# Sort by source: the last 96 of 416 steps placed by scattered transfers into a blanked array, the first 320 by products

## The chip, the cores and the metric

One core of a Trainium2 chip runs the whole program. The metric is the device time of one execution in microseconds. Engines go by the profile's short names: PE (TensorE, matrix products; PEld its weight loads), DVE (VectorE), ACT (ScalarE), POOL (GpSimd) and SP (SyncE, which mostly issues DMAs here).

## The reference

Four graph layers on 3125 nodes of 256 features and 53125 edges, cut to what matters here:

```python
x = layernorm(x + L0(x, src, dst, ...))          # max over the edges of each source node, 3 times
x = layernorm(x + L1(x, edge_index, type, weight, ...))   # relational layer, sum over the edges of each target, 2 times
x = layernorm(x + L2(x, edge_index, ...))        # normalised graph convolution
x = layernorm(x + L3(x, src, dst, ...))          # attention over the edges, then a feed-forward part
# in L0:
xi, xj = x[src], x[dst]
e = relu((xj - xi) @ theta.T + xi @ phi.T)
agg = jax.ops.segment_max(e, src, num_segments=N)
```

Nothing is said on the order of the edges, which come sorted by target. For the maximum over the edges of a source the kernel sorts them by source on the chip, and then walks along them.

## The kernel before

**The layout.** The edges are padded to SLOTS = 128 x 416 = 53248. An array of one value per edge lies in SBUF as 128 partitions x STEPS = 416 columns; edge number e is at partition e // 416 ("block"), column e % 416 ("step").

**The sort by source** is a counting sort. `edge_order` (from L204) compares and counts (L227 to L341, up to about 313 us), then looks up for each edge the place that it gets in the sorted order (the phase from L386, 313 to 405 us; its loops are on DVE, ACT and PE alone). `node_ends` (from L483) finishes the places in a run of short DVE instructions, each waiting for the one before: `place` is a number of 0 to 53247 for each edge, and `locate` splits it into `blk` (place // 416) and `stp` (place % 416). No two edges have the same place.

**The placing.** `permute` (from L531) then moves what is to be sorted, the other end's node number in two pieces (`env.piece`: number >> 8 and number & 255), to its place by matrix products. For each of the 416 columns t of the unsorted array, a one-hot matrix `hot_step` (128 x 416, L562) has the new column of the partition's edge, and for each piece a matrix `marked_piece` (128 x 128) has the piece's value at the new partition. Their product, added up in PSUM over all t (L607, banks 0 and 1), is the sorted array: in each element one of the 53248 summands isn't zero. `BySource.place_edges` (L704 to L714) joins the two banks to `self.row` = 256 x bank 0 + bank 1.

The columns are taken in groups of four (`group` = 4), in a ring of four groups. DVE makes for each group four `hot_step`, three `hot_block` (L565) and the fourth column's two `marked_piece` (L569); ACT makes the other three columns' six `marked_piece` (L589); PE does eight products (L607). DVE waits for `used` from four groups back, ACT for `hot`, PE for `hot` and `marked`. Each engine loops with `over_groups`. With 416 columns that is 104 groups, 26 rounds of the ring. POOL and SP have no work in this phase.

`permute` is called a second time in `node_ends`, for the ends of the nodes (25 columns, groups of one). `segments` and everything later follow.

**What sets the order.** Each `phase` ends with a barrier of all engines, then a block in which POOL resets the DMA state and clears the phase's semaphores one by one (L74), so no work of one phase overlaps with that of the next.

The array `flat`, a scratch tensor of 2 x SLOTS 4-byte elements in HBM, is used later by `StepOrder` only.

## Time and profile before

| | |
|---|---|
| median of 3 runs | 7662.52 us (7645.81 to 7680.71) |
| profiled execution | 7700.27 us |
| its span in the profile | 7698.5 us |
| PE busy | 3055.6 us (40%) |
| DVE busy | 3786.4 us (49%) |
| ACT busy | 1760.0 us (23%) |
| POOL busy | 3188.1 us (41%) |
| `permute` of the edges | 418 to 618 us of the span |
| granted clock of PE, mean | 0.685 |

Busy time is that of instructions on an engine; matmuls are pipelined and their ends modelled. All rows below are of one profiled execution, with times in microseconds from the span's start. "Idle before" is how long the engine stood still before an instruction, and what follows the arrow is what ended that. An instruction with "issue" there waited for nothing that the profile shows. DVE and ACT instructions overlap with the next of their engine, so the time from one start to the next is shorter than the duration. A DMA issued by POOL shows as DMA_INDIRECT, which is the time in which POOL makes the descriptors; the data move later.

### The profile page before, as it was taken

To read this page: it belongs to the slowest core of one execution; us is meant where nothing else is said; L and a number is where in the kernel's file an instruction comes from. 1 tells how busy PE (TensorE), PEld (TensorE's weight loads), DVE (VectorE), ACT (ScalarE), POOL (GpSimd) and SP (SyncE) were. 2 spreads that over 40 slices of the span, in tenths; PEclk is the share of its full clock that TensorE was granted. 3 is DMA by queue.
4 is the path that set the end of the run, shared out by engine and by line. 5 is a ranking of instruction groups with operands and counts; after the bars stand their busy time and mean duration, and the time that the engine had idled before them with its cause. 6 is when DMAs were issued, how large, how long until landed. Compare 5 with 4: busy or idle time off the path is not lost. (4 is left out here: it accounts for less than half of the span.)

```text
span 7698.5 us, 78156 instructions
## 1 busy us (share of the span) xinstructions
PE 3055.6 (40%) x12869; PEld 1815.1 (24%) x12895; DVE 3786.4 (49%) x9263; ACT 1760.0 (23%) x4531; POOL 3188.1 (41%) x3220
## 2 busy tenths in 40 slices
PE   4474000433335545689200199000200035666638
PEld 3332000221113222334100044000100024545415
DVE  8995445344444555544333444333543354555451
ACT  1182000021112444321222211222200011222211
POOL 0003666434443655300566400666366644444520
PEclk9997555655557777789655599555555558887769
DMA  0003455333333444333345333455245536777630
GB/s 7 0 0 99 163 168 176 102 107 128 124 127 103 142 144 152 111 113 149 134 172 172 133 146 137 151 175 175 102 148 184 173 114 202 252 246 246 214 79 17
DMA packets 376598, 1056.27 MB, mean 137 GB/s; under 512 B 73683, under 2 KB 161141, under 8 KB 329877
## 3 DMA queue, kind: packets, MB, share of 16 engines
q0 software_dynamic: 164688, 466.32, 20.4%
q1 hardware_dynamic: 210450, 587.55, 20.0%
q10 hardware_dynamic: 1330, 0.99, 0.0%
q8 instruction: 43, 0.70, 0.0%
q14 instruction: 87, 0.70, 0.0%
HBM read 537.47 MB, written 517.10 MB: 137 GB/s over the span
## 5 line engine op out<-in xcount | busy, mean ns | idle before, releaser
L912 POOL DMA_INDIRECT rows<-typed_table,index x832 | 826.9, 994 | 1324.1 <-DVE index L936 1085.8
L912 POOL DMA_INDIRECT out_of<-table,index x936 | 940.8, 1005 | 955.1 <-DVE index L936 679.0
L912 POOL DMA_INDIRECT rows<-table,index x728 | 722.6, 993 | 466.3 <-DVE index L936 242.5
L1086 PE MATMUL bank<-ident,tail 128*128 128x128 f32 x6 | 2.0, 434 | 1850.4 <-PEq L74 1850.4
L2276 PE MATMUL bank<-weights,out_of 128*128 128x512 f32 x1600 | 699.8, 595 | 26.7 <-DVE weights L2324 26.7
L2680 POOL DMA_INDIRECT qv<-qv_table,index x416 | 421.5, 1013 | 455.2 <-DVE index L2880 330.2
L930 ACT ACTIVATE rows<-rows,by_target_weight 128x256 f32<-128x256 f32 x832 | 345.7, 495 | 941.1 <-DMA rows<-typed_table,index 863.5
L951 DVE SCALAR_TENSOR_TENSOR y<-y,by_source_anew,out_of 128x256 f32<-128x256 f32 x897 | 434.1, 484 | 214.8 <-issue 86.5
L1806 PE MATMUL bank<-x,marks 128*128 128x416 f16 x1664 | 379.7, 389 | 390.7 <-ACT marks L1820 330.3
L1820 ACT ACTIVATE marks<-hot_block,x 128x128 f16<-128x128 f16 x1248 | 370.7, 387 | 409.6 <-DVE marks L1861 388.6
L951 DVE SCALAR_TENSOR_TENSOR out_of<-out_of,by_target_keep,rows 128x256 f32<-128x256 f32 x598 | 290.4, 486 | 306.4 <-issue 187.1
L1086 PEld LDWEIGHTS bank<-ident,tail 128*128 128x128 f32 x6 | 0.9, 203 | 1852.4 <-issue 1852.4
L2276 PEld LDWEIGHTS bank<-weights,out_of 128*128 128x128 f32 x1600 | 305.6, 191 | 391.4 <-issue 389.0
L2757 PE MATMUL bank<-weighed_rows,hot 128*128 128x272 f32 x832 | 283.6, 466 | 183.5 <-ACT y L2855 100.8
L2897 DVE TENSOR_TENSOR qv<-qv,bank 128x512 f32<-128x512 f32 x208 | 141.8, 685 | 377.6 <-remote 152.7
L2296 DVE COPY staged<-bank 128x512 f32<-128x512 f32 x200 | 138.4, 692 | 371.5 <-PE bank L2276 371.5
L1806 PEld LDWEIGHTS bank<-x,marks 128*128 128x128 f16 x1664 | 177.8, 109 | 592.6 <-issue 505.1
L951 DVE SCALAR_TENSOR_TENSOR state<-state,by_target_keep,rows 128x256 f32<-128x256 f32 x273 | 132.5, 485 | 366.2 <-issue 242.8
L2745 PE MATMUL bank<-near,y 128*128 128x256 f32 x832 | 253.1, 445 | 147.5 <-DMA near<-k_rows 108.0
L2296 ACT COPY staged<-bank 128x512 f32<-128x512 f32 x200 | 117.2, 586 | 637.6 <-PE bank L2276 637.6
L2855 ACT COPY y<-bank 128x272 f32<-128x272 f32 x416 | 153.5, 387 | 469.1 <-PE bank L2757 187.5
L1940 POOL MEMSET floor<- 128x256 f32 x1 | 0.3, 312 | 615.4 <-POOLq L74 615.4
(509 smaller groups left out, 6962.3 us busy)
## 6 DMA issues: line engine op xcount, KB each, us to landing
states<-y SPq DMA_DIRECT2D x156, 1024.0 KB
typed_table<-staged SPq DMA_DIRECT2D x400, 256.0 KB, 2.0
states<-state SPq DMA_DIRECT2D x78, 1024.0 KB
states<-out_of SPq DMA_DIRECT2D x78, 1024.0 KB
wide_states<-y SPq DMA_DIRECT2D x52, 1088.0 KB
near<-k_rows SPq DMA_DIRECT2D x416, 128.0 KB
out_of<-table,index POOLq DMA_INDIRECT x936
rows<-typed_table,index POOLq DMA_INDIRECT x832
```

Source lines behind the costliest of these rows:

```text
L912: pool.indirect_dma_start(out=rows[h][:, u * D:(u + 1) * D], out_offset=None, in_=table, in_offset=bass.IndirectOffsetOnAxis(ap=index[h][: ...
L930: nc.scalar.activation(row, row, ACT.Copy, scale=order.weight[:, bass.ds((RING * i + h) * GROUP + u, 1)]).then_inc(weighed, 1)
L951: nc.vector.scalar_tensor_tensor(out=state[h][:, u * D:(u + 1) * D], in0=before, scalar=marks[:, bass.ds(g * GROUP + u, 1)], in1=rows[h][: ...
L1806: last = nc.tensor.matmul(env.bank[i][:, 0:STEPS], self.marks[h][i][:, u * P:(u + 1) * P], self.hot_step[h][:, u * STEPS:(u + 1) * STEPS], ...
L1820: last = nc.scalar.activation(self.marks[h][i][:, u * P:(u + 1) * P], self.hot_block[h][:, u * P:(u + 1) * P], ACT.Copy, scale=self.pieces ...
L2276: last = nc.tensor.matmul(bank[:, 0:pair], turned_y[:, a * D + s * P:a * D + (s + 1) * P], weights[h][:, s * pair:(s + 1) * pair], start=s ...
L2296: copy(staged[m % slots][:], env.bank[a % banks][:, 0:pair]).then_inc(read, 1)
L2680: pool.indirect_dma_start(out=qv[b][:, u * PAIR:(u + 1) * PAIR], out_offset=None, in_=qv_table, in_offset=bass.IndirectOffsetOnAxis(ap=ind ...
L2745: last = nc.tensor.matmul(env.bank[k % 2][:, j * D:(j + 1) * D], hot_turned[h][:, u * P:(u + 1) * P], near[h][:, u * D:(u + 1) * D], start ...
L2757: nc.tensor.matmul(env.bank[2 + j][:, 0:ROW], hot[b % RING][:, u * P:(u + 1) * P], weighed_rows[b % 2][:, u * ROW:(u + 1) * ROW], start=Tr ...
L2855: nc.scalar.copy(staged[h][:, u * ROW:(u + 1) * ROW], env.bank[2 + u % 2][:, 0:ROW]).then_inc(kept, 1)
L2897: nc.vector.tensor_tensor(out=q, in0=q, in1=by_step(env.bank[k % 2][:], D, 2), op=ALU.mult).then_inc(multiplied, 1)
```

## The change

The first 320 columns of the unsorted array are placed by products as before (BY_PRODUCT). The last 96 go another way. In the look-up phase POOL blanks a tile, and SP stores it over the first SLOTS elements of `flat` (`slots`), 208 KB. `node_ends` makes two more tiles of 96 columns with DVE: `spot`, the place as a whole number, and `value`, 256 x piece 0 + piece 1. In the `permute` phase POOL issues 96 indirect DMAs, one for each of the columns; each sends 128 elements of 4 bytes, one of a partition, to their places in `slots`. SP waits for all of them (semaphore `scattered`), loads `slots` into the tile `scattered_in` and waits for that. `place_edges` then adds `scattered_in` to PSUM bank 1 where it copied bank 1 before. Both calls of `permute`, and the look-up phase, get two more semaphores each.

```diff
@@ -201,7 +201,10 @@
                 then(nc.vector.tensor_copy(env.piece[1][:], part[:]))
 
 
-def edge_order(nc, env, order, target, given):
+BY_PRODUCT = 320
+
+
+def edge_order(nc, env, order, target, given, slots):
 
 
 
@@ -381,9 +384,20 @@
             part = buffer(inner, nc, "part", 2 * W1)
             high_low = buffer(inner, nc, "high_low", 2 * W2, BF16)
             found = buffer(inner, nc, "found", 2 * W2)
-            names = ("added", "cut_high", "cut", "looked_up", "picked", "placed", "held")
-            with phase(nc, *names) as (added, cut_high, cut, looked_up, picked, placed, held), \
+            blank = buffer(inner, nc, "blank", STEPS)
+            names = ("added", "cut_high", "cut", "looked_up", "picked", "placed", "held", "blanked", "cleared")
+            with phase(nc, *names) as (added, cut_high, cut, looked_up, picked, placed, held, blanked, cleared), \
                     nc.Block() as block:
+                @block.gpsimd
+                def _(pool):
+                    pool.memset(blank[:], 0.0).then_inc(blanked, 1)
+
+                @block.sync
+                def _(sp):
+                    sp.wait_ge(blanked, 1)
+                    sp.dma_start(slots.rearrange("(p t) o -> p (t o)", t=STEPS), blank[:]).then_inc(cleared, 16)
+                    sp.wait_ge(cleared, 16)
+
                 def part_of(h):
                     return bulk(part[:, h * W1:(h + 1) * W1], GROUP)
 
@@ -477,10 +491,10 @@
         counting.close()
 
 
-        node_ends(nc, env, order, place, rank)
-
-
-def node_ends(nc, env, order, place, rank):
+        node_ends(nc, env, order, place, rank, slots)
+
+
+def node_ends(nc, env, order, place, rank, slots):
 
 
     with ExitStack() as inner:
@@ -491,6 +505,8 @@
         l_blk, l_stp = si("l_blk", TILES), si("l_stp", TILES)
         last, crosses = si("last", TILES), si("crosses", TILES)
         blk, stp = si("blk", STEPS), si("stp", STEPS)
+        spot = buffer(inner, nc, "spot", STEPS - BY_PRODUCT, I32)
+        value, scattered_in = si("value", STEPS - BY_PRODUCT), si("scattered_in", STEPS)
         with phase(nc, "step") as (step,), nc.Block() as block:
             @block.vector
             def _(dve):
@@ -507,6 +523,9 @@
                 then(nc.vector.tensor_tensor(out=place[:], in0=place[:], in1=blk[:], op=ALU.mult))
                 then(nc.vector.tensor_scalar(out=place[:], in0=place[:], scalar1=ROUND, scalar2=-ROUND, op0=ALU.add, op1=ALU.add))
                 then(nc.vector.scalar_tensor_tensor(out=place[:], in0=place[:], scalar=-1.0, in1=rank[:], op0=ALU.add, op1=ALU.subtract))
+                then(nc.vector.tensor_copy(spot[:], place[:, BY_PRODUCT:]))
+                then(nc.vector.scalar_tensor_tensor(out=value[:], in0=env.piece[0][:, BY_PRODUCT:], scalar=256.0, in1=env.piece[1][:, BY_PRODUCT:],
+                                                    op0=ALU.mult, op1=ALU.add))
                 locate(place, blk, stp)
                 locate(order.start, n_blk, n_stp)
                 then(nc.vector.tensor_scalar(out=order.some[:], in0=order.count[:], scalar1=1.0, scalar2=None, op0=ALU.min))
@@ -523,12 +542,12 @@
                 then(nc.vector.scalar_tensor_tensor(out=l_blk[:], in0=l_blk[:], scalar=1.0, in1=crosses[:], op0=ALU.add, op1=ALU.mult))
                 then(nc.vector.tensor_scalar(out=order.end_block[:], in0=l_blk[:], scalar1=-1.0, scalar2=None, op0=ALU.add))
 
-        order.place_edges(nc, env, place, blk, stp)
+        order.place_edges(nc, env, place, blk, stp, (spot, value, slots, scattered_in))
         permute(nc, env, n_blk, n_stp, [order.some], TILES, 1)
         segments(nc, env, order)
 
 
-def permute(nc, env, blk, stp, pieces, tiles, group):
+def permute(nc, env, blk, stp, pieces, tiles, group, scatter=None):
 
     n = len(pieces)
     body = RING * group
@@ -550,7 +569,23 @@
         hot_step = buffer(stack, nc, "hot_step", body * STEPS, BF16)
         hot_block = buffer(stack, nc, "hot_block", body * P, BF16)
         marked_piece = buffer(stack, nc, "marked_piece", body * n * P, BF16)
-        with phase(nc, "hot", "marked", "used", "held") as (hot, marked, used, held), nc.Block() as block:
+        with phase(nc, "hot", "marked", "used", "held", "scattered", "reloaded") as (hot, marked, used, held, scattered, reloaded), nc.Block() as block:
+            if scatter is not None:
+                spot, value, slots, scattered_in = scatter
+                many = STEPS - tiles
+
+                @block.gpsimd
+                def _(pool):
+                    for t in range(many):
+                        pool.indirect_dma_start(out=slots, out_offset=bass.IndirectOffsetOnAxis(ap=spot[:, t:t + 1], axis=0),
+                                                in_=value[:, t:t + 1], in_offset=None).then_inc(scattered, 16)
+
+                @block.sync
+                def _(sp):
+                    sp.wait_ge(scattered, 16 * many)
+                    sp.dma_start(scattered_in[:], slots.rearrange("(p t) o -> p (t o)", t=STEPS)).then_inc(reloaded, 16)
+                    sp.wait_ge(reloaded, 16)
+
             @block.vector
             def _(dve):
                 def make(g, h):
@@ -703,13 +738,13 @@
 
 class BySource(Order):
 
-    def place_edges(self, nc, env, place, blk, stp):
-        permute(nc, env, blk, stp, env.piece, STEPS, 4)
+    def place_edges(self, nc, env, place, blk, stp, scatter):
+        permute(nc, env, blk, stp, env.piece, BY_PRODUCT, 4, scatter)
         with phase(nc, "step") as (step,), nc.Block() as block:
             @block.vector
             def _(dve):
                 then = counted_steps(dve, step)
-                then(nc.vector.tensor_copy(env.tmp[:], env.bank[1][:, 0:STEPS]))
+                then(nc.vector.tensor_tensor(out=env.tmp[:], in0=env.bank[1][:, 0:STEPS], in1=scatter[3][:], op=ALU.add))
                 then(nc.vector.scalar_tensor_tensor(out=self.row[:], in0=env.bank[0][:, 0:STEPS], scalar=256.0, in1=env.tmp[:],
                                                     op0=ALU.mult, op1=ALU.add))
 
@@ -3342,7 +3377,7 @@
             edge_buffers(inner, nc, env)
             env.piece = [buffer(inner, nc, f"piece{i}", STEPS) for i in range(2)]
             edge_columns(nc, env, given["src"], given["dst"])
-            edge_order(nc, env, by_source, by_target, given)
+            edge_order(nc, env, by_source, by_target, given, flat[0:SLOTS, :])
         by_source.end_row, by_target.end_row = (buffer(stack, nc, "end_row", ROWS, BF16) for _ in range(2))
         steps = StepOrder(stack, nc, env, by_source, by_target, flat, window_table, k_rows)
         x, y = buffer(stack, nc, "x", TILES * D), buffer(stack, nc, "y", TILES * D)
```

## Rows read from the trace of the kernel before

**Rows 1.** Busy time by stage: stretch, length, busy and count per engine, clock, DMA.

```profile
core 0: us, PE busy (x) PEld busy (x) DVE busy (x) ACT busy (x) POOL busy (x), PEclk, DMA share, GB/s
313.00:405.50 92.50, 56.69 (x416) 42.41 (x416) 81.27 (x208) 19.20 (x52) 0.00 (x0) 1.00 0.00 0
418.00:616.00 198.00, 163.04 (x824) 73.77 (x824) 196.01 (x936) 193.28 (x624) 0.00 (x0) 1.00 0.00 0
```

**Rows 2.** Groups, 417.5 to 618 us: busy, mean ns of one, idle before, releasers.

```profile
L589 ACT ACTIVATE marked_piece<-hot_block,piece 128x128 bf16<-128x128 bf16 x624 | 193.4, 389 | 21.6 <-DVE marked_piece L569 19.1 <-issue 0.4
L607 PE MATMUL bank<-hot_step,marked_piece 128*128 128x416 bf16 x832 | 164.6, 342 | 49.4 <-ACT marked_piece L589 49.3
L562 DVE TENSOR_SCALAR hot_step<-iota_steps,stp 128x416 bf16<-128x416 f16 x416 | 133.7, 321 | 0.9 <-PEq L74 0.9
```

**Rows 3.** Timeline of the placing stage: start, duration, instruction, idle before it.

```profile
418.04 0.33 DVE L562 TENSOR_SCALAR hot_step<-iota_steps,stp 128x416 bf16<-128x416 f16 x1 [0.92 <-PEq L74]
...
500.49 0.53 DVE L569 TENSOR_SCALAR marked_piece<-iota_p,blk,piece 128x128 bf16<-128x128 bf16 x2
...
502.38 0.53 DVE L569 TENSOR_SCALAR marked_piece<-iota_p,blk,piece 128x128 bf16<-128x128 bf16 x2
...
616.26 1.57 PE L607 MATMUL bank<-hot_step,marked_piece 128*128 128x416 bf16 x8 [0.32 <-ACT marked_piece L589]
618.74 0.59 DVE L712 COPY tmp<-bank 128x416 f32<-128x416 f32 x1 [4.69 <-PEq L74]
```

**Rows 4.** Groups of GpSimd, whole span: a 4-byte gather, a 1 KB scatter.

```profile
L2547 POOL DMA_INDIRECT k_rows<-staged_k,step_place x25 | 24.7, 988 | 39.1 <-DVEq L2607 39.1
L2685 POOL DMA_INDIRECT ahead<-window_table,step_step_in x25 | 24.0, 962 | 7.6 <-issue 7.6
```

**Rows 5.** DMA: queue over 7284 to 7288 us (packets, MB, share); issues (KB, landing us).

```profile
q0 software_dynamic: 93, 0.00, 1.7%
...
typed_table<-staged SPq DMA_DIRECT2D x400, 256.0 KB, 2.0
...
weights<-in_L_gnn_thetas SPq DMA_DIRECT2D x3, 256.0 KB, 2.8
```

**Rows 6.** L1857 beside and without indirect DMAs: timeline, line (min/median/max), group.

```profile
2613.29 2.25 DVE L1857 TENSOR_SCALAR x<-iota_steps,x 128x416 f16<-128x416 f16 x8
2614.50 0.94 POOL L912 DMA_INDIRECT out_of<-table,index  x1 [0.30 <-issue]
2622.26 1.17 POOL L912 DMA_INDIRECT out_of<-table,index  x1 [3.52 <-DVE index L936]
2622.51 1.98 DVE L1857 TENSOR_SCALAR x<-iota_steps,x 128x416 f16<-128x416 f16 x8
3186.13 1.99 DVE L1857 TENSOR_SCALAR x<-iota_steps,x 128x416 f16<-128x416 f16 x8
...
L1857 DVE TENSOR_SCALAR x<-iota_steps,x x8: 310/323/518, 2613.3 to 2615.2; 128x416 f16<-128x416 f16 x8
...
L1857 DVE TENSOR_SCALAR x<-iota_steps,x 128x416 f16<-128x416 f16 x416 | 109.3, 334 | 0.0
```

**Rows 7.** Timeline: an indirect DMA beside a long DVE instruction.

```profile
744.78 1.49 POOL L912 DMA_INDIRECT out_of<-table,index  x1 [0.30 <-issue]
745.12 1.03 DVE L1457 TENSOR_SCALAR x<-tmp 128x416 bf16<-128x416 int32 x1
```

**Rows 8.** Timeline of node_ends: its first instruction, and two of 25 columns.

```profile
406.51 2.75 DVE L506 RECIPROCAL blk<-col_a 128x416 f32<-128x416 f32 x1 [1.09 <-PEq L74]
...
412.82 0.18 DVE L501 TENSOR_SCALAR n_blk<-by_source_start 128x25 f32<-128x25 f32 x1
413.04 0.18 DVE L502 TENSOR_SCALAR n_blk<-n_blk 128x25 f32<-128x25 f32 x1
```

**Rows 9.** Waits of SP's queue: total us, times, longest.

```profile
SPq L386 <- PEq L386: 92.1, 1, 92.1
SPq L74 <- PEq L74: 50.1, 44, 3.3
```

## The prediction

> **What bounds the stretch now.** I read the table of busy time by stage first, because an average over 7698.5 us says nothing of one stage. The change touches the sort of the edges by source, which fills the first 634 us. In its placing stage, 418 to 616 us, VectorE is busy 196.0 us of 198.0, ScalarE 193.3, TensorE 163.0 and GpSimd 0.0, and the DMA engines move nothing [rows 1]. The groups of instructions of this stage come next. ScalarE's 624 scalings are busy 193.4 us and wait 21.6 before them, 19.1 of which is the wait for the first group; TensorE waits 49.4 us for ScalarE [rows 2]. So TensorE isn't the bound. VectorE and ScalarE are, nearly tied, and neither waits for the other. The timeline has the pace. The last instructions of two groups of four steps, the pair of L569, start at 500.49 and 502.38 us, 1.885 us apart; a check over the stage gives the same: 196.0 / 104 groups = 1.885 [rows 1, 3]. ScalarE needs 193.4 / 104 = 1.86 us a group [rows 2]. The first L562 starts at 418.04, the last product starts 616.26 and ends 617.83, and the next instruction on VectorE follows at 618.74 [rows 3]. All later work waits for it, since every phase ends in a barrier. A microsecond saved here is a microsecond of the whole.
>
> **Part 1, fewer products.** 416 steps become 320, so 104 groups become 80 and the loop of 26 rounds of four groups becomes 20 without a rest. 24 groups x 1.885 us = **45.2 us** less, on VectorE and ScalarE alike, and TensorE's share goes with them (its eight products take 1.57 us of the 1.885) [rows 1, 3]. What would be next to bound the stage if these were cheaper doesn't matter: their pace per group stays.
>
> **Part 2, 96 scatters on GpSimd.** Each sends 128 values of 4 bytes. The trace has a near twin, L2685: 25 gathers of 4-byte elements, written out without a loop, 962 ns each with 7.6 / 25 = 0.30 us between them; a scatter exists too, L2547, 988 ns with rows of 1 KB [rows 4]. The time follows the count of 128 addresses and hardly the size or the direction, so one costs 0.96 + 0.30 = 1.26 us and 96 of them 121 us. GpSimd idles in this stage, so from 418.3 they are issued by 539. The reload of 208 KB follows. A load of 256 KB takes 2.8 us to land [rows 5], and the last scatter has to land before it, in some 2 us more (an estimate from the 2.0 us of a store there), so `reloaded` stands at about 544. The products end at 617.8 - 45.2 = 572.6 at the earliest. The scatters are hidden with 29 us to spare. They surface only if one costs more than (572.6 + 9.6 - 418.3 - 5) / 96 = 1.65 us, the 9.6 being part 3. SP, whose queue waits behind `scattered`, has nothing else queued until the phase's end.
>
> The transfers' own cost: four 4-byte gathers put 1.7% on the 16 engines in 4 us, 1.1 us of engine time over all of them, under 0.1 us per engine for four [rows 5]. The trace has no scattered 4-byte write into HBM. From below it costs what the gather does. From above it costs 2.0 us with no overlap, the time in which a 256 KB store lands [rows 5]. The gather is the nearer row, so I take hidden.
>
> The Trainium skill ("DMA: Bandwidth & Descriptors", Specifications) says that below 512 bytes a DMA engine reads, modifies and writes. No row here shows that for a 4-byte write; it is what would push toward the upper bound, which is rival B.
>
> **Part 3, what the scatters do to VectorE.** This is the term that I am least sure of. The stage has no GpSimd work now, so I looked where the same sort of VectorE instruction runs beside indirect DMAs. L1857 is the twin of L562: 128x416, 16 bits in and out, eight in a row. Undisturbed, eight take 1.99 us. At 2613.29 they take 2.25, and one of the eight lasts 518 ns where its median is 323; GpSimd's DMA of 2614.50 lies in the burst and takes 0.94 us, no longer than alone [rows 6]. So GpSimd gets through short VectorE instructions, and makes one of them wait 0.20 to 0.26 us at times. How often: over all 416, L1857's mean is 334 ns against 321 for L562, 13 ns x 416 = 5.4 us [rows 2, 6]. Starts in a burst are (1.99 - 0.32) / 7 = 0.24 us apart, so the bursts cover 100 us; at one DMA per 1.26 us that is at most 80, so at least 0.07 us each; leaving out the bursts in which GpSimd pauses, like 3186.13, it is nearer 0.10. I take 0.10 x 96 = **9.6 us**. Bounds: 0 (each DMA slips in between), and 0.25 x 96 = 24 us. A gain is excluded, as nothing gets faster by sharing. ScalarE has only 0.02 us a group of slack, so it can't take up the loss, and it is paid in full.
>
> What GpSimd suffers: beside a long VectorE instruction it does wait. The DMA of 744.78 takes 1.49 us and ends 0.12 us after the 1.03 us instruction of 745.12 [rows 7]. The stage's instructions last 0.25 to 0.33 us and the next overlaps them, so I expect 0 to 0.1 us of such waiting, 120 to 130 us for all 96. It changes no end.
>
> **Part 4, small ones.** Two more VectorE instructions of 96 columns in the node_ends phase: the 25-column ones start 0.22 us apart and those of 416 columns last 0.59 [rows 3, 8], so about 0.27 each, **0.5 us**. The blanking (a memset on GpSimd, a 208 KB store on SP) lies in the look-up stage of 92.5 us in which GpSimd and DMA idle and SP waits 92.1 us for TensorE [rows 1, 9]; memset and store are a few us at its start, so it costs nothing. Without that cover it would cost some 4 us. The sum from PSUM replaces a copy of the same shape, 0.59 us before and after [rows 3]. Semaphores: the phase with seven leaves VectorE idle for 1.09 us, that with one for 0.92 [rows 3, 8], 0.03 each. Three phases get two more: **0.2 us**. The barrier on GpSimd after a phase with DMAs could take longer: the 44 barriers take 1.14 us on average and 3.3 at the longest [rows 9], so up to 2 us, and I take 0.
>
> **Sum.** -45.2 + 9.6 + 0.5 + 0.2 = -34.9 us. The profiled execution took 7700.27 us, span 7698.5, so it would take 7665.4. The median of the three runs is 7662.52, 38 below the profiled one; the same difference gives **7628 us**. With part 3's bounds and part 4's 2 us the forecast's own range is 7618 to 7644.
>
> **Rivals.**
> D, no disturbance: GpSimd fits between VectorE's instructions. For it: the burst of 2622.51, beside the DMA of 2622.26, takes 1.98 us. Against: the 518 ns instruction [rows 6]. -44.5 us, 7618.
> B, the scatters surface: at 1.9 to 2.0 us each, by slow 4-byte writes or by waits like 744.78's all along, the reload ends at 418.3 + 192 + 4 = 614 and the stage saves only 4 us: 7659. At 1.8 us it would be 7640. For it: no row of such a write, and [rows 7]. Against: [rows 4] and the idle DMA engines.
> A, starvation, which ends slower: VectorE is busy all through the stage, 196.0 of 198 us, and if its instructions in the fast mode kept GpSimd from writing descriptors, the 96 scatters would come after the last of them: 418 + 151 of products + 121 + 5 = 695 instead of 617.8, +77 us, 7740. It decides from where a third of the DMAs are still to come when the products end (578 + 40 + 5 = 623). For it: the stage has no gap, whereas the bursts of the twin last 2 us. Against: 2614.50, wholly inside a burst, isn't held at all.
> The Trainium skill ("SBUF — State Buffer", Who interferes with whom) states exactly this rule: a VectorE instruction in a two-port mode holds the shared port pair for its whole length and GpSimd blocks, starved of descriptor writes. This trace agrees for the long instruction of 745.12 and disagrees for the short ones of 2613.29.
>
> **Chances.** Forecast 0.55, D 0.20, B 0.17, A 0.08. The range, 7608 to 7664, takes in the forecast, D and B with the spread of the runs, and leaves out A and the tails. 0.5% (38 us) is about what a measurement can tell from no change; the border is 7624. Faster: 0.16 of D and 0.14 of the forecast, 0.30. Slower: A, 0.08. Within: 0.62.
>
> **What would show it.** L562 320 times, its pace still 1.885 us a group once GpSimd is done (after about 540) and about 2.0 before: each DMA costs 0.10 and 1.5 of them fall in a group. L562's mean 325 to 345 ns. 96 indirect DMAs at 1.25 to 1.35 us from one start to the next. The next stage begins about 583 instead of 618.7, on a release by TensorE and not by SP. Wrong, if SP's wait for `scattered` ends last, or if the mean of the DMAs is above 1.3 us.

## The result

The changed kernel took 7706.0 us at the median against 7651.7 for the kernel before: a ratio of 1.0084, interval 1.0058 to 1.011 (the plain quotient of the two medians is 1.0071). The prediction was 7628 and a ratio of 0.9955; it had given a chance of 0.08 to any loss over 0.5%. On a second sort of chip, reached only late in the study, the same two kernels stand at 0.994 (0.9926 to 0.9953). Most of this section is about how one change can be both.

The profiled execution of the changed kernel took 7682.64 us, its span 7680.9. First, the groups of its placing stage, as [rows 2] for the kernel before: busy us, mean ns of one, idle before them and its releasers. L597 is the former L562, L624 the former L589, L642 the former L607, and L580 the new scatters.

```profile
L624 ACT ACTIVATE marked_piece<-hot_block,piece 128x128 bf16<-128x128 bf16 x474 | 146.8, 388 | 133.4 <-DVE marked_piece L604 128.7 <-issue 3.2
L642 PE MATMUL bank<-hot_step,marked_piece 128*128 128x416 bf16 x624 | 133.1, 362 | 144.1 <-ACT marked_piece L624 106.0 <-issue 19.2 <-DVE marked_piece L604 18.9
L597 DVE TENSOR_SCALAR hot_step<-iota_steps,stp 128x416 bf16<-128x416 f16 x320 | 100.2, 313 | 111.1 <-remote 77.8 <-issue 29.6 <-PE bank L642 2.9
L580 POOL DMA_INDIRECT flat<-value,spot x96 | 93.2, 971 | 134.4 <-POOLq L74 105.4 <-issue 29.0
```

ScalarE waits 128.7 us for VectorE, TensorE 106.0 for ScalarE, and VectorE 111.1 us for something that the profile can't name ("remote", "issue"). None of the three is busy most of the time while the scatters are issued. In [rows 1] VectorE and ScalarE had worked 196.0 and 193.3 of 198.0 us. By stretches (length, busy and count of each engine, granted clock, DMA share and GB/s), the first two with scatters, the third after them:

```profile
core 0: us, PE busy (x) PEld busy (x) DVE busy (x) ACT busy (x) POOL busy (x), PEclk, DMA share, GB/s
418.00:486.00 68.00, 19.78 (x72) 8.25 (x72) 17.91 (x81) 16.53 (x54) 51.09 (x53) 0.71 0.02 1
486.00:554.00 68.00, 8.79 (x24) 3.06 (x24) 7.53 (x34) 5.58 (x18) 42.13 (x44) 0.53 0.03 4
554.00:681.00 127.00, 104.54 (x528) 47.39 (x528) 126.73 (x606) 124.79 (x403) 0.00 (x0) 0.98 0.00 0
```

Before 554 us, some 13 of the 80 groups of products are made in 136 us; after it, the other 67 in 127 us, 1.89 us each, the pace of before. The stage is close to GpSimd's 121 us plus the products' 151 us, as if the two excluded each other. Its first and last marks are the same as those of [rows 3]: 418.34 us for the first hot step and 685.58 for the instruction that reads PSUM (L747), 267.2 us long. In the kernel before it is 200.7. That is 66.5 us more, about the size of the loss (0.0084 x 7652 = 64 us; the medians lie 54 apart). The two profiled executions don't show the loss as a whole: the span of the changed kernel, 7680.9 us, is 17.6 shorter than the 7698.5 before, since its other stages were some 84 us shorter there. The idle time before the same 52 VectorE instructions in a later pass, for one, is 259.2 us in the trace before and 220.1 in this one. Whole times of single executions on this sort of chip thus differ by tens of us for reasons outside the change, and the stage is the surer measure. TensorE's granted clock averages 0.53 in the second stretch, near the lower of its two levels. It is busy there for 8.79 of 68 us, and was for 19.78 of the 68 before. Since it stands idle for most of both stretches, its products are no bound in them.

The timeline has the stall itself: start, duration, instruction, idle before it.

```profile
432.86 0.33 DVE L597 TENSOR_SCALAR hot_step<-iota_steps,stp 128x416 bf16<-128x416 f16 x1 [2.91 <-PE bank L642]
...
437.23 2.93 PE L642 MATMUL bank<-hot_step,marked_piece 128*128 128x416 bf16 x8 [3.51 <-ACT marked_piece L624]
...
446.28 0.33 DVE L597 TENSOR_SCALAR hot_step<-iota_steps,stp 128x416 bf16<-128x416 f16 x1 [11.26 <-issue]
...
450.47 2.93 PE L642 MATMUL bank<-hot_step,marked_piece 128*128 128x416 bf16 x8 [10.30 <-ACT marked_piece L624]
...
466.55 0.33 DVE L597 TENSOR_SCALAR hot_step<-iota_steps,stp 128x416 bf16<-128x416 f16 x1 [18.29 <-issue]
...
540.28 0.96 POOL L580 DMA_INDIRECT flat<-value,spot  x1 [0.30 <-issue]
...
542.45 0.35 SPq L586 DMA_DIRECT2D scattered_in<-flat  x1
...
552.66 0.33 DVE L597 TENSOR_SCALAR hot_step<-iota_steps,stp 128x416 bf16<-128x416 f16 x1 [16.86 <-remote]
```

TensorE's last product ends at 440.16 us by the profile, which models the ends of products; TensorE stands idle, and VectorE still waits until 446.2. The only thing that VectorE can be waiting for ahead of an L597 is `used`, the semaphore that the last product of each group raises, and that frees a quarter of the ring. Seven such waits last 110.2 us together, the longest five 16.9 to 20.4 us each. The last of them ends 11 us after the last scatter, and none follows. The trace also records when the semaphore `used` is raised, though not every time. Between 433 and 555 us it has 488.8, 511.2, 533.6 and 552.5 us, and then 554.0, 554.1 and 554.2, where by the profile groups of products end at 440.2, 453.4, 474.1, 496.2, 518.5 and 540.9. On the faster sort of chip, in the same stage, each recorded count lies within 0.1 us of the end of a group.

So the first theory (T) was: while GpSimd issues indirect DMAs one right after another, the count by which a finished product raises a semaphore arrives late, about one in 20 us (by the three times above, one in 22.4).

### The profile page after: what moved, and what is told of

It reads as the page before. It is cut to its first block and busy times, and to the rows that moved or that the text cites. A ratio compares the mean times of both kernels' runs of the same rounds, so it can differ in the third digit from the quotient of the medians.

```text
span 7680.9 us, 77013 instructions
## 1 busy us (share of the span) xinstructions
PE 3051.2 (40%) x12703; PEld 1808.6 (24%) x12703; DVE 3734.7 (49%) x9049; ACT 1714.2 (22%) x4387; POOL 3272.3 (43%) x3317
## 3 DMA queue, kind: packets, MB, share of 16 engines
q0 software_dynamic: 167760, 466.38, 20.3%
## 5 line engine op out<-in xcount | busy, mean ns | idle before, releaser
L986 DVE SCALAR_TENSOR_TENSOR y<-y,by_target_keep,rows 128x256 f32<-128x256 f32 x299 | 145.2, 485 | 224.9 <-issue 175.7
```

The lines of the kernel that those rows point to most:

```text
L986: nc.vector.scalar_tensor_tensor(out=state[h][:, u * D:(u + 1) * D], in0=before, scalar=marks[:, bass.ds(g * GROUP + u, 1)], in1=rows[h][: ...
```

## The experiments

Stage lengths run from the first hot step to the instruction that reads PSUM, as above. Where a kernel was executed only once there is no interval, and I go by the stage.

**Is it the issuing, and whose?** Four kernels, on a chip where the kernel before took 7652 us. The first leaves the scatters out (its result lacks the last 96 steps):

```diff
-                @block.gpsimd
-                def _(pool):
-                    for t in range(many): pool.indirect_dma_start(...).then_inc(scattered, 16)
...
-                    sp.wait_ge(scattered, 16 * many)
```

> The changed kernel without its 96 scatters (the last 96 columns are not placed at all; SP loads the blanked array at once). All theories: without GpSimd's transfers the placing stage holds its pace of 1.885 us per group from the first to the last, so it lasts 80 x 1.885 + 3 = 154 us instead of 267 in the changed kernel and 200 before. If it lasts longer than 160 us, the stall has nothing to do with the scatters but with the shorter loop or SP's block, and every theory falls.

The stage took 155.9 us, without a gap, 7588.1 us in all. That is 200.7 less 24 groups x 1.87. Part 1 of the prediction stands, and the scatters cost 111.4 us, which are the 110.2 of waits and 1 more.

The second gathers 4-byte elements in place of scattering them (it leaves the placing of the last 96 steps out), the third scatters rows of 1 KB from a zeroed tile into another array (and leaves it out too):

```diff
-   indirect_dma_start(out=slots, out_offset=...(ap=spot[:, t:t + 1], axis=0), in_=value[:, t:t + 1], in_offset=None)
+   indirect_dma_start(out=value[:, t:t + 1], out_offset=None, in_=slots, in_offset=...(ap=spot[:, t:t + 1], axis=0))   # second
+   indirect_dma_start(out=env.states, out_offset=...(ap=spot[:, t:t + 1], axis=0), in_=env.wide[:], in_offset=None)    # third
```

> Each scatter is replaced by a gather of 128 elements of 4 bytes from the blanked array, with the same addresses (the last 96 columns stay unplaced). Theory T (counts by which the products report their end arrive late while GpSimd issues indirect transfers, about one per 20 us): the direction doesn't matter, the stage lasts 255 to 275 us with VectorE idle for stretches of about 20 us. Rival W (slow scattered 4-byte writes into HBM hold something up): no such writes now, the stage lasts 154 to 170 us.

> Each scatter sends rows of 1 KB instead of 4 bytes, to the rows of a large scratch tensor with the same indices (the last 96 columns stay unplaced). It tells whether the size matters. Theory T, if it is the issuing that delays the counts: as with 4 bytes, stage 255 to 275 us. Rival C (16 completions within 0.2 us, since tiny transfers end all at once, crowd the semaphores): 1 KB rows spread them, the stage lasts 160 to 200 us. The prediction's own mechanism (port sharing between VectorE and GpSimd) would give 154 + 10 us for all sizes.

268.8 and 267.4 us, each with seven gaps, the longest 20.4 and 20.3 us. Direction, size and the small writes into HBM don't matter. The fourth issues 96 plain transfers of the same 128 x 4 bytes from SyncE in place of GpSimd's (and leaves the placing of those steps out):

```diff
+                    for t in range(many):
+                        sp.dma_start(env.other[t * P:(t + 1) * P, :], value[:, t:t + 1]).then_inc(scattered, 16)
```

> The 96 transfers are plain ones of 128 x 4 bytes issued by SP, to another part of the scratch array (the last 96 columns stay unplaced), with the same 16 counts each on the same semaphore; GpSimd does nothing. Theory T (it is GpSimd's issuing): no delay, 154 to 160 us. Rival C (it is the DMA's completion counts, whoever issues): the stage is stretched like the changed kernel's while they last, over 200 us if they last 100 us or more.

156.4 us, no gap, 7552.4 us. (The first of the four has the same stage and took 36 us more in all, which shows the spread of single executions.) SyncE issued its 96 in 52 us, twice as fast as GpSimd. As many transfers with as many counts of their own do no harm when GpSimd doesn't issue them. Whether plain transfers from GpSimd would do harm wasn't tried.

**Pauses, and two rivals of T.** Next to T stood: SyncE's long wait for 1536 counts is what disturbs; GpSimd's use of the port that it shares with VectorE is; or only VectorE sees the count late. These four ran where the kernel before took 7629 us. The first is complete, with batches:

```diff
                     for t in range(many):
+                        if t % 6 == 0:
+                            pool.wait_ge(hot, 5 * (t // 6) + 1)
```

> The changed kernel, complete, with GpSimd's scatters in sixteens of six: before each six it waits until VectorE has made another five groups (6 x 1.26 = 7.6 us of scatters in every 5 x 1.885 = 9.4 us), so it pauses about 1.8 us in each. Theory T (late counts while GpSimd issues back to back): the counts get through in the pauses, VectorE waits less than 5 us at a time, stage 160 to 200 us. If a pause of 1.8 us is too short for them, stage over 240 us, since VectorE's stalls stop GpSimd as well and both wait for each other's slow pace.

170.3 us and 7593.7 in all. GpSimd's timeline and VectorE's group show why:

```profile
449.22 1.22 POOL L582 DMA_INDIRECT flat<-value,spot  x1 [0.30 <-issue]
451.40 1.28 POOL L582 DMA_INDIRECT flat<-value,spot  x1 [0.96 <-DVE marked_piece L606]
...
467.84 0.95 POOL L582 DMA_INDIRECT flat<-value,spot  x1 [0.30 <-issue]
472.06 1.28 POOL L582 DMA_INDIRECT flat<-value,spot  x1 [3.26 <-DVE marked_piece L606]
```

```profile
L599 DVE TENSOR_SCALAR hot_step<-iota_steps,stp 128x416 bf16<-128x416 f16 x320 | 101.8, 318 | 7.6 <-remote 5.6 <-PE bank L644 1.1 <-PEq L74 0.9
```

Pauses of 1 to 3.3 us, fifteen of them, are enough: VectorE's waits sum to 7.6 us, none above 1.6. The last scatter ends at 580.3 us, after VectorE's last instruction of the stage (579.4), and the reload is issued at 581.5; so VectorE stands idle for 9.9 us ahead of the read of PSUM, where it is 4.7 in [rows 3]. (Expectations further on give 171.9 us for this stage; from the first hot step to the read of PSUM the trace has 170.3.)

The second has GpSimd wait for the 1536 counts, not SyncE:

```diff
+                    pool.wait_ge(scattered, 16 * many)
+                    pool.sem_inc(all_in, 1)
...
-                    sp.wait_ge(scattered, 16 * many)
+                    sp.wait_ge(all_in, 1)
```

> The changed kernel, complete, but GpSimd itself waits for the scatters' 1536 counts after its last one, and SP waits for one count of GpSimd's. Rival S (SP's waiting on a semaphore that is counted up 1536 times disturbs the others): nobody waits on it now while the scatters are issued, stage 154 to 170 us. Theory T: no difference to the changed kernel, 262 to 270 us.

269.0 us, the same gaps. SyncE's wait is not it. The third puts 96 memsets in the place of the scatters (and so leaves those steps out):

```diff
+                        pool.memset(wide[:], 0.0).then_inc(scattered, 1)
+                        pool.wait_ge(scattered, t + 1)
```

> GpSimd does 96 memsets of 128x1024 f32 instead of the scatters, each about as long, one after the other (the last 96 columns stay unplaced). Rival G (any busy GpSimd holds up the counts or the port): stage over 200 us. Theory T (it is the issuing of indirect transfers): stage 154 to 175 us, VectorE's instructions somewhat longer where the two meet at the port.

```profile
L598 DVE TENSOR_SCALAR hot_step<-iota_steps,stp 128x416 bf16<-128x416 f16 x320 | 159.7, 499 | 0.9 <-PEq L74 0.9
...
L581 POOL MEMSET wide<- 128x1024 f32 x96 | 95.5, 995 | 110.2 <-POOLq L74 104.7
```

The stage took 211.9 us, 56 more than without them. By the number alone that is the rival's outcome, over 200, and T's 154 to 175 was missed: the port's share was far larger than I had put. But the stage looks quite unlike the changed kernel: the hot steps last 499 ns on average in place of 313, and VectorE never waits (0.9 us). So a busy GpSimd that issues no DMAs lengthens VectorE's instructions and holds up no count, which I take for the sharing of the port. The changed kernel has short instructions and long waits.

The fourth lets TensorE's sequencer wait for the count of two groups back and then raise a semaphore of its own, `freed`, for VectorE:

```diff
-                        dve.wait_ge(used, g - RING + 1)
+                        dve.wait_ge(freed, g - RING + 1)
...
+                    if not isinstance(g, int) or g >= 2:
+                        pe.wait_ge(used, g - 1)
+                        pe.sem_inc(freed, 1)
```

> The changed kernel, complete, but VectorE doesn't wait on the count that the products' end makes. TensorE's own sequencer waits for it, two groups later, and then counts up another semaphore, on which VectorE waits. If the count itself is late (theory T, strict form), TensorE waits as long as VectorE did and the stage stays at 255 to 275 us. If it is VectorE's seeing of it that is late, the relay gets round it, 154 to 175 us.

```profile
PE bank L645 <- remote: 87.7, 6, 19.5
...
PE bank L645 <- issue: 19.5, 1, 19.5
```

269.0 us. Now TensorE itself waits 87.7 us in six waits for the count of products that by the profile it has long ended. The count itself is late, and not only VectorE's view of it.

**How long a pause, and how the loss grows.** On a third chip, where the kernel before took 7761 us. Two are complete with other batches, `t % 8` with `6 * (t // 8) + 1`, and `t % 4` with `3 * (t // 4) + 1`:

> The changed kernel complete, but GpSimd issues its 96 scatters in batches of eight, each batch held until VectorE has written six further groups' hot steps; the first batch goes at once. Eight scatters take 8 x 1.26 = 10.1 us and six groups 6 x 1.885 = 11.3, so GpSimd stands still for about 1.2 us in each batch. Theory T (the counts of completed products arrive late only while GpSimd issues DMAs one after another without a pause): a pause of about 1 us every ten lets them through, the placing stage takes 157 to 168 us and the kernel ends 35 to 45 us below the kernel before. Rival (a pause must be long, or it is the total of the issuing that counts): the stage stays near 267, the kernel some 50 us slower than before.

> The same in batches of four scatters for every three groups: 5.0 us of issuing and 5.65 us of groups, so a pause of about 0.6 us in each batch. Theory T: as with eight and six, stage 157 to 168 us, 35 to 45 us below the kernel before; if a pause of 0.6 us is too short, waits of some us return on VectorE and the stage lies between 170 and 267.

Stages of 202.6 and 190.1 us; VectorE's waits above 1 us sum to 40.5 and 30.1 (14 and 13 of them, at most 6.1 and 3.2 us). The pauses weren't those that I had planned. With eight in a batch GpSimd paused after every batch, for 1.07 to 9.88 us, longer than the batches of six did, and waits came all the same. With four in a batch, 11 of the 23 gaps between batches were 0.31 us, which is no pause, and the other 12 lasted 1.0 to 5.3; so batches ran together into runs of eight and more. What the two share, and the batches of six lack, are runs of some 10 us or more without a pause. My first figure for theory T, a pause of "about 1 us every ten", was wrong. In time the two stood at 0.9972 (0.9953 to 0.9991) and 0.9971 (0.995 to 0.9992). For the first, whose stage is 1.9 us longer than that of the kernel before, I can't account for that gain of 7 to 36 us; it remains open.

The third has `BY_PRODUCT = 368` and 48 scatters back to back, the fourth rings of eight buffers in place of four:

> The changed kernel with 368 steps by products and 48 by scatters, all 48 back to back. Theory T (a loss for each us in which GpSimd issues without a pause, the groups going on at their own pace before and after): GpSimd is busy for 60 us, the groups that get through in it are as many as the first 60 us of the changed kernel held, and the stage takes about 60 + 11 us and some 84 groups x 1.885 = 229 us. Rival (a fixed cost of starting the scatters): the stage is as long as the changed kernel's, 267, plus 12 groups x 1.885 = 290.

> The changed kernel with rings of eight buffers in place of four for the hot steps of the edges' placing. Theory T (the count of a group's products comes at one per some 22 us while GpSimd issues): VectorE runs four groups further ahead once and then stands still as before, so the stage is shorter by about four groups x 1.885 = 8 us, near 260. Rival (the counts are late by a fixed delay of some 20 us, not rationed): eight buffers let twice as many groups be under way in each delay, and the stage falls to about 210 us.

The half took 230.8 us (7804.4 in all), against 229 by T and 290 by the rival. Its gaps of 3.8, 17.6, 18.7 and 10.8 us end at 487.8, some 7 us after the last scatter. The loss goes with the time in which GpSimd issues. The rings gave 258.6 us (7779.5) against 260 by T and 210 by the rival: the counts are rationed, not delayed by a fixed time, and the deeper ring moves the first long wait from 435 to 485 us. Its timeline shows more than that. Between 445 and 485 us, where VectorE and TensorE still have work that waits for no count, their instructions themselves are held apart:

```profile
450.71 0.33 DVE L599 TENSOR_SCALAR hot_step<-iota_steps,stp 128x416 bf16<-128x416 f16 x1 [1.14 <-issue]
450.71 0.51 PE L644 MATMUL bank<-hot_step,marked_piece 128*128 128x416 bf16 x1 [2.31 <-issue]
...
452.11 0.25 DVE L602 TENSOR_SCALAR hot_block<-iota_p,blk 128x128 bf16<-128x128 bf16 x1 [1.07 <-issue]
452.11 0.10 PEld L644 LDWEIGHTS bank<-hot_step,marked_piece 128*128 128x128 bf16 x1 [2.69 <-issue]
...
453.51 0.33 DVE L599 TENSOR_SCALAR hot_step<-iota_steps,stp 128x416 bf16<-128x416 f16 x1 [1.15 <-issue]
453.51 0.51 PE L644 MATMUL bank<-hot_step,marked_piece 128*128 128x416 bf16 x1 [2.29 <-issue]
...
456.49 1.86 ACT L626 ACTIVATE marked_piece<-hot_block,piece 128x128 bf16<-128x128 bf16 x6 [9.42 <-remote]
```

VectorE starts one instruction in 1.40 us, and TensorE one in 1.40 us too, a weight load and a product by turns. ScalarE waits 9.42 us for a count that VectorE's last instruction of the group gives, which ended at 447.47: here VectorE's counts are late as well. A group has eight weight loads and eight products, and 16 x 1.40 = 22.4 us is the distance between the waits' ends in the changed kernel. So what is rationed isn't the products' count alone but, as far as these rows show, one instruction of TensorE in 1.40 us, whether it gives a count or not. In the changed kernel the eight products of a group still start within 2.5 us, and only their count comes late, so some instructions can run ahead of the ration. T named the sign that shows with a short ring and not the whole of it. Every execution here was recorded by the profiler, with a record of each instruction; whether that recording has a part in the holding, none of the runs can tell.

**Does it hold elsewhere?** The kernel before has the same signs in its gather passes, where GpSimd issues for more than half of the time (422 of 731 us in the pass of L1358). The groups of L1358 and L2897 in the first trace:

```profile
L2897 DVE TENSOR_TENSOR qv<-qv,bank 128x512 f32<-128x512 f32 x208 | 141.8, 685 | 377.6 <-remote 152.7 <-PE bank L2745 146.7 <-issue 77.6
...
L1358 DVE TENSOR_TENSOR hot_block<-iota_p,x 128x1024 f16<-128x1024 bf16 x52 | 63.5, 1222 | 259.2 <-remote 252.1 <-PE bank L1806 7.1
```

Four kernels ran on the next chip: the kernel before for a trace, the batches of six, the kernel before with a pause in the gathers, and batches of six with `BY_PRODUCT = 328` and so 88 scatters.

> The kernel before itself, for a trace of it on the same chip as the runs beside it: its placing stage should take 200 to 203 us as in the first trace. If it takes over 220, the stage itself differs from chip to chip and the lengths of earlier stages on that chip must be read against it.

> The changed kernel complete, with GpSimd's scatters in batches of six, one batch for every five groups of products (the edit that gave a placing stage of 171.9 us). Theory T: the whole gain of the change comes back, so against the kernel before 29 us less in the stage, a ratio of about 0.9962. Rival (the stage's time is given back further on): a ratio of 1.000, with the stage as short.

> As the batches of six per five groups, but 328 steps by products and 88 by scatters: 82 groups, the last batch due at group 71 rather than 76, so that the last DMA and the reload come before the products end. Theory T: stage = 82 x 1.885 + 11 + some 3 us of short waits = 168 us, against 171.9 with 320 steps; ratio to the kernel before 0.996. Rival: if the tail was not the reload's, 171.9 + 2 x 1.885 = 175.7.

That chip was of another sort. The kernel before took 6584.8 us on it, 14% less than on any chip so far, and its trace has the same groups so:

```profile
L2897 DVE TENSOR_TENSOR qv<-qv,bank 128x512 f32<-128x512 f32 x208 | 141.7, 683 | 170.5 <-PE bank L2745 165.6 <-DMA qv<-qv_table,index 2.0
...
L1358 DVE TENSOR_TENSOR hot_block<-iota_p,x 128x1024 f16<-128x1024 bf16 x52 | 63.3, 1216 | 0.0
```

The instructions last as long as before (1216 against 1222 ns, 683 against 685), the placing stage takes the same 200.7 us, and the waits put down to "remote" are gone. This chip has no late counts. The batches of six took 161.8 us and 0.993 (0.9913 to 0.9947), the 328 steps 160.7 and 0.9937 (0.9915 to 0.9958). The pause in the gathers was this:

```diff
                             in_offset=bass.IndirectOffsetOnAxis(ap=index[h][:, u:u + 1], axis=0)).then_inc(gathered[h], 16)
+                    pool.wait_ge(gathered[h], (i + 1) * (16 * GROUP))
```

> The kernel before, with no scatters in the stage, and one wait more on GpSimd in the gather passes: after each group of eight gathers it waits until they have landed, some 2 to 3 us without an issue. Theory T (counts of finished TensorE work are late wherever GpSimd issues back to back): VectorE's idle time ahead of the target sort's hot blocks (242 us put down to a semaphore from elsewhere) falls to under 100, and the kernel is up to 100 us faster, less what the later gathers cost. Rival (that idle time is the gathers' own, or the semaphore there is another): the idle time stays above 200 us and the kernel is slower by the pauses, 150 groups x 2 us at most.

A ratio of 1.1192 (1.1174 to 1.1211), 789 us more. As this chip has no late counts, it says nothing on T. It shows the price of such a pause where GpSimd is the bound: 2496 gathers are 312 groups of eight, 2.5 us each, and the idle time ahead of the three groups of L912 rose from 1904 to 2695 us. My bound, 150 groups at 2 us each, had both factors too low. Whether shorter pauses pay in the gather passes of the slower chips wasn't tried.

**The changed kernel on the other sort.** As it was, with its scatters back to back:

> The changed kernel itself, back to back scatters. In the last job the kernel before took 6585 us where it took 7629 to 7761 elsewhere, and its trace there had no waits at all ahead of the hot blocks of line 1358, against 252 us in the first trace: late counts are a property of the chip as well. Theory T (late counts alone make the change a loss): on a chip where the kernel before takes about 6585 us, the placing stage has no long waits, takes 163 to 170 us, and the change is about 35 us faster, ratio 0.993 to 0.996; on a chip where it takes 7600 or more, the stage is near 267 us and the ratio about 1.008 again. Rival (the back to back scatters hurt everywhere, and only pacing helps): stage near 267 and ratio above 1.005 on either sort of chip.

Again a chip of the faster kind came up, with the kernel before at 6582.4 us. The changed one took 6540.2: 0.994 (0.9926 to 0.9953), 42 us less. The stage took 157.3 us. Its groups and two of its stretches:

```profile
L580 POOL DMA_INDIRECT flat<-value,spot x96 | 107.7, 1122 | 134.4 <-POOLq L74 105.5 <-issue 28.9
L597 DVE TENSOR_SCALAR hot_step<-iota_steps,stp 128x416 bf16<-128x416 f16 x320 | 100.9, 315 | 0.9 <-PEq L74 0.9
```

```profile
486.00:554.00 68.00, 55.90 (x286) 25.30 (x286) 68.00 (x323) 66.38 (x215) 53.60 (x48) 1.00 0.02 1
```

In the 68 us in which the first trace had 34 VectorE instructions, here are 323, and 48 scatters beside them. Theory T's condition is met, though its range for the stage, 163 to 170 us, was too high, and its rival, that back to back scatters hurt everywhere, falls.

**A schedule for both.** The 328 steps ran once more, on a chip of the slower sort (7644.9 us for the kernel before):

> The kernel with 328 steps by products and 88 scatters in batches of six for every five groups, again. On a chip of the slower sort (the kernel before at 7600 us or more) theory T expects what one look at 320 steps in such batches gave, a stage of about 172 us or a little less, against 201: ratio 0.995 to 0.997. On a chip of the faster sort (about 6585) it expects 0.993 to 0.994, as measured. Rival: on the slower sort the batches' pauses are not enough over many runs, and the ratio is 0.999 or above.

7614.8 us, 0.997 (0.9951 to 0.9989), the stage 167.6 us: 33 us less in the stage, and 8 to 37 in the kernel. This is the version to keep: it is faster than the kernel before on either sort of chip, while the change as made gains 0.6% on one and loses 0.8% on the other.

## Why the prediction was wrong

**Part 1 was right.** 24 groups gave 44.8 us without scatters (200.7 - 155.9), against 45.2, and the pace after the scatters is 1.89 us.

**Part 2 was right on the slow chip to about 2 us.** The scatters run from 419.1 to 541.2 us (the prediction had 418.3 to 539), 971 ns with 29.0 / 95 = 0.31 us between them, the reload is issued at 542.45. They would have been hidden, had the products gone on. On the faster chip, where VectorE is never idle, they take 1122 ns and end at 556.5 us, still hidden: the waiting that I put at 0 to 0.1 us was 0.15. From start to start that is 1.42 us, above the 1.35 that the prediction allowed, on the very chip on which its ratio nearly came out (0.994 against 0.9955). The gather of [rows 4] was the right twin in price.

**Part 3 is the step that failed.** The term of 9.6 us, bounded by 24, measured 111.4 (267.2 - 155.9 us), or 112.9 with both stages on one chip (268.8 - 155.9, with gathers in place of scatters). I asked what the scatters do to VectorE's instructions and found 9.6 us of disturbance, with bounds of 0 and 24. As a price of that mechanism it was too high: on the faster chip it is 157.3 - 155.9 = 1.4 us, or 0.015 us a scatter, though the 155.9 is from a chip of the other sort. What I left out was that the scatters could act on a wait. I reasoned that GpSimd's DMAs and VectorE meet at the memory port only, and bounded the cost by rows of instruction lengths. The rows of waits in the same windows would have shown more. The burst of 2613.29 in [rows 6], on which I rested the term, comes right behind this (timeline of the kernel before):

```profile
2607.62 5.79 PE L1806 MATMUL bank<-x,marks 128*128 128x416 f16 x32 [0.83 <-ACT marks L1820]
...
2612.15 1.23 DVE L1358 TENSOR_TENSOR hot_block<-iota_p,x 128x1024 f16<-128x1024 bf16 x1 [7.20 <-remote]
```

VectorE had stood still for 7.20 us just before the burst that I measured, on a semaphore that the profile couldn't attribute, and over all 52 of them for 252.1 us, in 23 waits. An unattributed wait of that size, in a pass in which GpSimd's DMAs and a ring between VectorE and TensorE run together, was the nearest row to the new stage. GpSimd is busy for 422 us of that pass; scaled to its 93 us here the wait gives 252 x 93 / 422 = 56 us, an estimate, which is half of what came and more than twice my upper bound. Why the instructions are held, and so why the term is 111 us and not another number, stays open.

**Part 4 was right or too small to see.** The first hot step starts at 418.34 us in place of 418.04, 0.3 us later, with the blanking and the two new instructions before it.

**The rivals.** D (no disturbance, -44.5 us) is what the faster chips do: -43.4 in the stage, -31 to -49 in the kernel. B didn't occur. A, the starvation, has the right sign and nearly the right size (+77 against +66.5 in the stage) by luck, since it too added GpSimd's time to that of the products, but with the parties the wrong way round: GpSimd was never held, it held the others. I had argued against A with a DMA that wasn't delayed inside a burst; that was true, and of no help. The Trainium skill ("SBUF — State Buffer", Who interferes with whom) has VectorE's two-port instructions blocking GpSimd; with VectorE busy for 68.00 of 68 us, GpSimd got 48 scatters through at 1122 ns, so where the instructions are short, a block costs a DMA 0.15 us and no DMA is starved. The other direction, the memsets' 0.58 us of VectorE's time each, the trace with the memsets shows.

**The signs I named** held in part: 320 hot steps, 96 DMAs within 1.25 to 1.35 us from start to start, 1.89 us a group once GpSimd was done. Others failed: the hot steps' mean was 313 ns and not 325 to 345, so even the disturbance of Part 3 didn't show in their lengths; the next stage began at 685.6 us and not 583; and the pace before 540 was not 2.0 but over 10 us a group, which is what pointed to the error. Neither of the two that I had named as "wrong, if" came true on the slow chip, so they didn't cover the way in which the prediction failed.

## What to carry to other kernels

Before giving idle GpSimd a run of indirect DMAs, look at which engines in that stage pass buffers through a short ring, and search the trace for such a ring beside such DMAs: read the waits there, those put down to nobody above all, and not only the lengths of the instructions. Issue the DMAs in small batches tied to the progress of the work beside them, six for every five groups of 1.885 us here: on the slower chips that turned +66 us in the stage into -30 to -33, and on the faster ones it cost some 4 us of the gain. Look at the pauses that the DMAs really had, since GpSimd's waits for the other engines shift them. And where a gain of half a per cent decides, measure on more than one chip, with the kernel before beside it each time.

## What the runs showed of the hardware

- Chips differ by more than the change. In six groups of runs, each on one chip, the kernel before took 7652, 7629, 7761 and 7645 us on four chips and 6585 and 6582 on two. Between the traces of the two sorts the instructions of L1358 and L2897 agree within 0.5% and L562 within 2% (321 and 316 ns), and the placing stage without scatters takes 200.7 us on both; what differs is the waiting while GpSimd issues.
- On the slower sort, back to back indirect DMAs of GpSimd at one per 1.26 us (scatters of 4 bytes and of 1 KB, gathers of 4 bytes) ration the counts of finished groups of products to one per 22.4 us, after some 11 us in which nothing is seen. In the changed kernel the counts that VectorE gives ScalarE and ScalarE gives TensorE arrive at once in the same stretch, and so does the one that TensorE's sequencer gives in the relay. With rings of eight, where more instructions are ready, VectorE and TensorE start one instruction each per 1.40 us, and VectorE's count reaches ScalarE some 9 us late. As many DMAs from SyncE do nothing of the kind, nor do memsets on GpSimd.
- A pause of about 1 us after every six DMAs, with one of 3 us now and then, lets nearly all counts through (7.6 us of waits). With eight in a batch, and pauses of 1.07 to 9.88 us, or with batches of four of which about half ran together, part of the waits returns (40 and 30 us). Why instructions and counts are held, and why only on some chips, none of these runs can tell.
- A GpSimd memset of 128x1024 in fp32 (995 ns) costs VectorE 0.58 us in this stage; a scatter of 128 elements on the faster sort, about 0.02 ((157.3 - 155.9) / 96).
